# Third attention layer: raw keys loaded in a head's second step, score operands in its third, with the band sum, the values and the masked keys placed anew on GpSimd

## The chip, the cores and the metric

The kernel runs as one program on one core of a Trainium2 chip. The metric is the device time of one execution in microseconds (us). A core has TensorE (PE), VectorE (DVE), ScalarE (ACT), GpSimd (POOL) and SyncE (SP), each with an instruction stream of its own; they meet at semaphores. In this kernel SP issues the DMA transfers, and sixteen DMA engines carry them out.

## The reference

Eight layers one after another work on x, four sequences of 512 tokens with 128 channels: attention and feed-forward in turn, each between layer norms and with a residual. The change touches the third attention layer alone (L2_attn):

```python
qkv = (x @ w_qkv.T).reshape(B, N, 3, H, hd).transpose(2, 0, 3, 1, 4)     # B 4, N 512, H 16, hd 8
q, k, v = (qkv[0] * scale, qkv[1], qkv[2])
attn = jnp.einsum('bhid,bhjd->bhij', q, k)
idx = (clip(j - i, -31, 31) + 31)                                          # 63 buckets
qL = jnp.einsum('bhid,hdm->bhim', q, rpe_k_table)
attn = attn + jnp.take_along_axis(qL, idx, axis=-1)
kL = jnp.einsum('bhjd,hdm->bhjm', k * scale, rpe_q_table)
attn = attn + jnp.swapaxes(jnp.take_along_axis(kL, idx, axis=-1), 2, 3)
attn = jax.nn.softmax(attn, axis=-1)
out = jnp.einsum('bhij,bhjd->bhid', attn, v)
S = segment_sum(attn, idx)                                                 # over j, into 63 buckets
out = out + jnp.einsum('inbh,hnd->bhid', S, rpe_v_table)
return out.transpose(0, 2, 1, 3).reshape(B, N, C) @ w_proj.T + b_proj
```

The relative terms differ from a constant only within 31 tokens of the diagonal, so the kernel computes them on a band of three 32-wide blocks around it.

## The kernel before, in words

`l2_attn` (L2053) works through 16 heads. A head has eight steps (PAIRS = 8), and a step treats two of the sixteen 32-token query blocks of all four sequences at once, 128 partitions by two times 512 keys. Every engine runs its own loop over the step number t, with h = t // 8 the head and i = t % 8 the step in the head, and what each engine does in which step is written out by hand; the text calls (h, i) step i of head h. Only semaphores tie the loops together.

In a step, TensorE computes the scores of two blocks (L2668 to L2673) into one of two PSUM slots, VectorE adds the band `qb` to them (L2523) and takes the maximum (L2525), ScalarE exponentiates them into `pr` (L2606), and VectorE transposes the probabilities of the step before (L2532). Three steps and more later TensorE multiplies them with the values (L2702). The band of a head goes three ways round:

- Query side: TensorE (L2636) computes it two heads ahead, ScalarE copies it out (L2585), SP stores it to DRAM (`q_store`, L2373) and loads it back skewed by one element per row (`q_load`, L2380) into `qb`.
- Key side: SP loads the head's eight rows of raw keys, repeated over 16 shifts, into the single buffer `rawk` (`keys`, L2336) and a table of shifts (L2340). GpSimd multiplies the raw keys with a mask into the single buffer `xk` (`expand`, L2462), TensorE multiplies them with the shifts in steps 1 to 3 (L2649), and ScalarE copies the product to `kb` (L2592). `combine` on GpSimd masks the far part of `qb` (L2470) and adds `kb` (L2472).
- Probability side: SP stores the band part of `pr` to DRAM four times a head (`p_store`, L2391 to L2397) and loads it back skewed twice a head (`s_load`, L2404) into `sb`. GpSimd zeroes what lies outside (`cut`, L2477), VectorE transposes it (L2538), TensorE multiplies it with the value table (L2715).

Score operands of a head (`head_scores`, L2347 to L2351: queries and keys split into bf16 parts, and a row of constants) are loaded one head ahead, the value table too (`head_values`, L2357). `values` on GpSimd (L2448, L2452) spreads the next head's values over the four sequences.

All DMAs of the loop are issued by SP on its one queue, in program order, and SP stands still at each wait. Its steps before the change: `p_store` in even steps (it waits for ScalarE), `s_load` in steps 3 and 7 (it waits at L2403 until the store issued three steps earlier has landed), `q_load` of the next head and `q_store` of the one after in step 0, `head_scores` of the next head in step 3, `keys` of head h+2 in step 4 (waits for `xk_ready`, signalled by `expand` of head h+1), `head_values` in step 5. GpSimd's: `sums` in steps 1 and 5, `cut` in 2 and 6, `combine` of the next head in 4, `values` of the next head in 5 (waits for `pv_done`, which TensorE signals in its step 4), `expand` of head h+2 in 7.

The skewed loads read DRAM through

```python
pitch = width + GRP
return bass.AP(band.tensor, band.offset + offset, [[GRP * pitch, B], [pitch + step, GRP], [1, width]])
```

with B = 4 and GRP = 32, while the raw keys' source has 16 as its first dimension: `[[0, HALF], [T * P, HD], [1, T * P]]`.

Of the kernel before, what the change touches and what calls it, by code (L numbers as in the profile page):

```python
# [22 lines left out]
HEADS, HD = 16, 8  # L23
# [2029 lines left out]
def l2_attn(nc, xs, c, w, scratch):  # L2053
# [4 lines left out]
    with ExitStack() as ctx:  # L2058
# [269 lines left out]
        with nc.Block() as block:  # L2328
            @block.sync
            def _(sp):  # L2330
                def keys(h):

                    if h:
                        sp.wait_ge(m["xk_ready"], h)
                    src = bass.AP(k32.tensor, k32.offset + h * HD * T * P, [[0, HALF], [T * P, HD], [1, T * P]])
                    sp.dma_start(rawk[:, :], src).then_inc(m["kl"], 16)  # L2336
                    if h >= 2:
                        sp.wait_ge(m["l_ps"], ROUND["k", h - 2, KEY_ROUNDS - 1])
                    src = bass.AP(rel_d.tensor, rel_d.offset + h * HD * KEY_SHIFTS, [[1, HALF], [KEY_SHIFTS, HD], [1, WINDOW_COLS]])
                    sp.dma_start(kshift[h % 2][:, :], src).then_inc(shifts_loaded[h % 2], 16)  # L2340
# [12 lines left out]
                def head_values(h):  # L2353

                    if h >= 2:
                        sp.wait_ge(m["o_ps"], 2 * h - 2)
                    sp.dma_start(rvt[h % 2][:, :, :].rearrange("p k n -> p (k n)"), rv_d[h]).then_inc(rv_slot_loaded[h % 2], 16)  # L2357
# [24 lines left out]
                def p_store(o):  # L2382
                    n, u = o // 2, 4 * (o % 2)
                    sp.wait_ge(m["p_ready"], 4 * o + 4)
                    if n >= PBAND_RING and o % 2 == 0:
                        before = n - PBAND_RING
                        sp.wait_ge(s_read[before % 2], 16 * (before // 2 + 1))
                    dst = pband[n % PBAND_RING][:, GRP:].rearrange("p (a c) -> p a c", c=BAND)
                    src, sem = pr[o % PR_RING], p_stored[o % PR_RING]
                    if o % 4 == 0:  # L2390
                        sp.dma_start(dst[:, 0, GRP:], src[:, 0, GRP:BAND]).then_inc(sem, 16)  # L2391
                        sp.dma_start(dst[:, 1:4, :], src[:, 1:4, 0:BAND]).then_inc(sem, 16)
                    elif o % 4 == 3:
                        sp.dma_start(dst[:, u:u + 3, :], src[:, 0:3, 0:BAND]).then_inc(sem, 16)
                        sp.dma_start(dst[:, u + 3, 0:2 * GRP], src[:, 3, 0:2 * GRP]).then_inc(sem, 16)
                    else:
                        sp.dma_start(dst[:, u:u + 4, :], src[:, :, 0:BAND]).then_inc(sem, 16)  # L2397

                def s_load(n):
                    for o in (2 * n, 2 * n + 1):  # L2400
                        sp.wait_ge(p_stored[o % PR_RING], p_stores(o))
                    if n >= 2:
                        sp.wait_ge(m["st_ready"], n - 1)  # L2403
                    sp.dma_start(sb[n % 2][:, :, :].rearrange("p a n -> p (a n)"), skewed(pband[n % PBAND_RING], 1, 1, HROW)).then_inc(s_read[n % 2], 16)  # L2404
# [14 lines left out]
                for t in range(L2_STEPS + 4):  # L2419
                    h, i = t // PAIRS, t % PAIRS  # L2420
                    if t % 2 == 0 and 0 <= (t - 2) // 2 < L2_STEPS // 2:
                        p_store((t - 2) // 2)
                    if t % 4 == 3 and 0 <= (t - 7) // 4 < 2 * HEADS:
                        s_load((t - 7) // 4)
                    if i == 0 and h + 1 < HEADS:
                        q_load(h + 1)
                    if i == 0 and 3 <= h + 2 < HEADS:
                        q_store(h + 2)
                    if i == 3 and 2 <= h + 1 < HEADS:
                        head_scores(h + 1)  # L2430
                    if i == 4 and h + 2 < HEADS:
                        keys(h + 2)
                    if i == 5 and 2 <= h < HEADS:
                        head_values(h)

            @block.gpsimd
            def _(g):
                g.memset(ones3[:, :], 1.0).then_inc(m["ones_ready"], 1)
                g.memset(xk[:, 0:GRP], 0.0).then_inc(m["once_ready"], 1)
                g.memset(xk[:, GRP + T * P:], 0.0).then_inc(m["once_ready"], 1)  # L2440

                def values(h):

                    if h:
                        g.wait_ge(m["vd_ready"], h)
                    if h >= 2:
                        g.wait_ge(m["pv_done"], 2 * h - 2)
                    g.tensor_tensor(vs[:, :, :, :], va[:, :, h, :].unsqueeze(1).broadcast_to([P, 2, NB, HD]),  # L2448
                                    rvf[:, :, h, :].unsqueeze(2).broadcast_to([P, 2, NB, HD]), ALU.add).then_inc(m["vs_ready"], 1)
                    g.wait_ge(m["vs_ready"], h + 1)  # L2450
                    for v in range(2):
                        last = g.tensor_tensor(vd[h % 2][:, v, :, :].rearrange("p k (b d) -> p k b d", d=HD),  # L2452
                                               vs[:, v, :, :].unsqueeze(2).broadcast_to([P, NB, B, HD]),
                                               of_batch.unsqueeze(1).unsqueeze(3).broadcast_to([P, NB, B, HD]), ALU.mult)
                    last.then_inc(m["vd_ready"], 1)

                def expand(h):

                    g.wait_ge(m["kl"], 16 * (h + 1))
                    if h:  # L2460
                        g.wait_ge(m["l_ps"], ROUND["k", h - 1, KEY_ROUNDS - 1])
                    g.tensor_tensor(xk[:, GRP:GRP + T * P].rearrange("p (g c) -> p g c", c=HALF), rawk[:, :].rearrange("p (g c) -> p g c", c=HALF),  # L2462
                                    own_shift.unsqueeze(1).broadcast_to([P, T * P // HALF, HALF]), ALU.mult).then_inc(m["xk_ready"], 1)

                def combine(h):

                    g.wait_ge(qband_read[h % 2], 16 * (h // 2 + 1))
                    g.wait_ge(m["l_ready"], ROUND["k", h, KEY_ROUNDS - 1])
                    far = qb[h % 2][:, :, 2 * GRP:]
                    g.tensor_tensor(far, far, reached.unsqueeze(1).broadcast_to([P, NB, GRP]), ALU.mult).then_inc(m["added"], 1)  # L2470
                    g.wait_ge(m["added"], h + 1)
                    g.tensor_tensor(qb[h % 2][:, :, :], qb[h % 2][:, :, :], kb[:, :, :], ALU.add).then_inc(m["comb_ready"], 1)  # L2472

                def cut(n):

                    g.wait_ge(s_read[n % 2], 16 * (n // 2 + 1))
                    g.tensor_tensor(sb[n % 2][:, :, 0:GRP], sb[n % 2][:, :, 0:GRP], inside.unsqueeze(1).broadcast_to([P, NB // 2, GRP]),  # L2477
                                    ALU.mult).then_inc(m["masked"], 1)

                def sums(n):  # L2480

                    g.wait_ge(m["p_ready"], 8 * n + 8)
                    if n >= 4:
                        g.wait_ge(m["u_ps"], n - 3)
                    g.tensor_tensor(sm[:, n % 4, :, :, :], rs[:, n % 2, :].rearrange("p (g a) -> p a g", a=NT).unsqueeze(3).broadcast_to([P, NT, 2, B]),
                                    of_batch.unsqueeze(1).unsqueeze(1).broadcast_to([P, NT, 2, B]), ALU.mult).then_inc(m["sm_ready"], 1)

                expand(0)
                values(0)
                combine(0)  # L2490
                expand(1)
                values(1)
                for t in range(L2_STEPS + 12):
                    h, i = t // PAIRS, t % PAIRS
                    if t % 4 == 1 and 0 <= (t - 5) // 4 < 2 * HEADS:
                        sums((t - 5) // 4)
                    if t % 4 == 2 and 0 <= (t - 10) // 4 < 2 * HEADS:
                        cut((t - 10) // 4)
                    if i == 4 and h + 1 < HEADS:
                        combine(h + 1)  # L2500
                    if i == 5 and 2 <= h + 1 < HEADS:
                        values(h + 1)
                    if i == 7 and h + 2 < HEADS:
                        expand(h + 2)
                ln.powers(g, 2 * B, start=B)

# [780 lines left out]
```

## Time and profile before

| | us |
|---|---|
| median of 3 runs | 2629.41 (2624.09 to 2635.16) |
| profiled execution | 2632.55 |
| its span, first to last instruction | 2630.6 |
| PE / DVE / ACT / POOL busy | 1926.2 / 1713.3 / 1090.8 / 847.6 |
| the layer's stage, about | 1555 to 2085 |

A line of instruction groups gives busy time, mean duration and idle time before them, with what ended it. In the waits, "A <- B" means that A stood idle until B's result came. The DMA share is the mean busy share of the sixteen DMA engines. A DMA issued by SP counts from its issue to its landing, when its semaphore is complete; a DMA "issue" on SP takes about half a microsecond of SP itself.

### The profile page before, as it was taken

How to read it: one execution, taken by the hardware profiler on the slowest of the kernel's cores; microseconds unless marked ns; L12 is line 12 of the kernel's file. 1: busy time of each engine (PE TensorE's matmuls, PEld its weight loads, DVE VectorE, ACT ScalarE, POOL GpSimd, SP SyncE). 2: the span in 40 equal slices, each digit the busy share in tenths (PEclk: the TensorE clock that was granted, in tenths of full speed). 3: DMA queues.
4: the chain of work that ended last, by engine and by line, in shares of the span. 5: the costliest groups of instructions: out<-in, count | busy, mean ns of one | idle time of the engine just before them, and what ended most of it. 6: DMA issues, size and time to landing. Idle time of an engine off the chain costs nothing. (4 is left out here: it accounts for less than half of the span.)

```text
span 2630.6 us, 46533 instructions
## 1 busy us (share of the span) xinstructions
PE 1926.2 (73%) x16472; PEld 1324.4 (50%) x16472; DVE 1713.3 (65%) x4060; ACT 1090.8 (41%) x2021; POOL 847.6 (32%) x627
## 2 busy tenths in 40 slices
PE   4888886387777784559999647787787549995446
PEld 1555554155555553437777524454454338884334
DVE  3777776576555554659999843788888672224564
ACT  1666663254544442204444223555555213331332
POOL 3000000574444421014444334445545169201001
PEclk8999999699999987659999765898988669997667
DMA  3011110210000000010000065566665140000000
GB/s 100 29 38 39 39 39 3 63 27 15 15 15 15 15 15 5 1 21 11 20 20 20 11 192 140 164 177 172 173 173 153 48 175 17 16 0 8 0 1 19
DMA packets 126467, 145.04 MB, mean 55 GB/s; under 512 B 72472, under 2 KB 100171, under 8 KB 123490
## 3 DMA queue, kind: packets, MB, share of 16 engines
q1 hardware_dynamic: 123040, 132.95, 18.1%
q10 hardware_dynamic: 3266, 9.96, 1.0%
q8 instruction: 99, 1.62, 0.3%
q14 instruction: 62, 0.51, 0.1%
HBM read 94.59 MB, written 40.81 MB: 51 GB/s over the span
## 5 line engine op out<-in xcount | busy, mean ns | idle before, releaser
L407 ACT ACTIVATE l0a_pr<-l0a_sm,l0a_nm 128x512 f32<-128x512 f32 x256 | 184.9, 723 | 147.4 <-DVE l0a_nm L324 146.9
L324 DVE CUSTOM_DVE_ANT_0 l0a_sm<-l0a_ps_s,l0a_tb 128x512 f32<-128x512 f32 x256 | 171.0, 685 | 93.9 <-PE l0a_ps_s L473 90.8
L2606 ACT ACTIVATE l2a_pr<-l2a_ps_s,l2a_nm 128x512 f32<-128x512 f32 x256 | 174.1, 687 | 120.8 <-DVE l2a_nm L2525 119.9
L481 PE MATMUL l0a_ps_p<-top_c_ident,l0a_pr 128*128 128x128 f32 x1024 | 170.4, 290 | 54.2 <-ACT l0a_pT L415 54.1
L481 PEld LDWEIGHTS l0a_ps_p<-top_c_ident,l0a_pr 128*128 128x128 f32 x1024 | 110.0, 143 | 117.1 <-ACT l0a_pr L407 64.7
L2525 DVE TENSOR_REDUCE l2a_nm<-l2a_ps_s 128x2 f32<-128x1024 f32 x128 | 156.7, 1224 | 4.4
L2532 DVE STREAM_TRANSPOSE l2a_tt<-l2a_pr 128x1024 f32<-128x1024 f32 x128 | 158.0, 1234 | 0.1
L1508 POOL TENSOR_TENSOR l1f_h<-l1f_lm,l1f_sg 128x512 f32<-128x512 f32 x72 | 92.6, 1286 | 184.0 <-DVE l1f_lm L1577 184.0
L754 POOL TENSOR_TENSOR l0f_ct<-l0f_raw,l0f_cos_scaled 128x1024 f32<-128x1024 f32 x32 | 76.3, 2386 | 184.1 <-issue 94.7
L1880 ACT ACTIVATE l2f_h<-l2f_ps_h 128x512 f32<-128x512 f32 x128 | 76.7, 599 | 134.7 <-PE l2f_ps_h L1425 128.9
L1635 ACT ACTIVATE l1f_csb<-l1f_ps_c,l1f_b3e 128x512 f32<-128x512 f32 x128 | 88.2, 689 | 104.9 <-PE l1f_ps_c L1425 104.6
L1918 PEld LDWEIGHTS l2f_ps_y<-l2f_w2T,l2f_h 128*128 128x128 f32 x1024 | 119.1, 192 | 2.6
L2702 PE MATMUL l2a_ps_o<-l2a_tt,l2a_vd 128*32 128x256 f32 (+7 forms) x1472 | 119.8, 364 | 0.0
L1918 PE MATMUL l2f_ps_y<-l2f_w2T,l2f_h 128*128 128x128 f32 x1024 | 119.3, 275 | 0.0
L1838 DVE SCALAR_TENSOR_TENSOR l2f_acc<-l2f_ps_y,l2f_comb,l2f_acc 128x128 f32<-128x128 f32 x112 | 31.6, 344 | 133.1 <-PE l2f_ps_y L1918 132.9
L990 PE MATMUL l0f_ps_side<-l0f_wqkv,l0f_hT 128*128 128x512 f32 x192 | 109.8, 663 | 11.5 <-ACT l0f_hT L905 10.8
L2523 DVE TENSOR_TENSOR l2a_ps_s<-l2a_ps_s,l2a_qb 128x192 f32<-128x192 f32 (+2 forms) x160 | 45.7, 303 | 106.2 <-PE l2a_ps_s L2673 61.3
L286 POOL COPY l0a_vh<-l0a_va 128x128 f32 x14 | 4.1, 296 | 333.2 <-PE l0a_ps_o L492 333.2
L473 PE MATMUL l0a_ps_s<-l0a_ks,l0a_qs 48*128 48x512 bf16 x256 | 101.7, 398 | 10.1 <-issue 9.5
L2649 PE MATMUL l2a_ps_l<-l2a_xk,l2a_kshift 128*32 128x256 f32 x768 | 71.3, 504 | 48.7 <-POOL l2a_xk L2462 46.2
L770 POOL TENSOR_TENSOR l0f_rn<-l0f_ss,top_c_half 128x16 f32<-128x16 f32 x32 | 95.0, 2968 | 33.1 <-DVE l0f_ss L854 32.1
L2462 POOL TENSOR_TENSOR l2a_xk<-l2a_rawk,l2a_masks 128x2048 f32<-128x2048 f32 x16 | 72.3, 4517 | 66.0 <-DMA l2a_rawk<-l_k 66.0
(501 smaller groups left out, 5220.9 us busy)
## 6 DMA issues: line engine op xcount, KB each, us to landing
l2a_rawk<-l_k SPq DMA_DIRECT2D x16, 1024.0 KB, 13.2
l2a_qb<-l_qband SPq DMA_DIRECT2D x16, 768.0 KB
l2a_sb<-l_pband SPq DMA_DIRECT2D x32, 384.0 KB
l_qband<-l2a_staged SPq DMA_DIRECT2D x14, 768.0 KB, 15.4
l0a_tb<-l_bias SPq DMA_DIRECT2D x16, 448.0 KB
l2a_ks<-l_k SPq DMA_DIRECT2D x16, 384.0 KB
l_pband<-l2a_pr SPq DMA_DIRECT2D x32, 192.0 KB, 9.4
l_pband<-l2a_pr SPq DMA_DIRECT2D x32, 144.0 KB, 2.9
```

Source lines behind the costliest of these rows:

```text
L324: v.tensor_tensor_reduce(sm[j % 4][:, :], ps_s[j % 2][:, :], tb[slot][:, off:off + N][:, ::-1], -1.0, 3e38, ALU.add, ALU.min, nm[:, j % 4: ...
L407: a.activation(pr[j % 4][:, :], sm[j % 4][:, :], ACT.Exp, bias=nm[:, j % 4:j % 4 + 1], scale=-1.0).then_inc(m["p_ready"], 1)
L473: pe.matmul(ps_s[j % 2][:, :], qs[slot][:, b * N + it * P:b * N + (it + 1) * P], ks[slot][:, b * N:(b + 1) * N], start=True, stop=True).th ...
L481: last = pe.transpose(ps_p[j % 2][:, tile(k)], pr[j % 4][:, tile(k)], ident[:, :])
L770: g.tensor_tensor(rn[:, u, :], ss[:, u, :], c["half"][:, :], ALU.pow).then_inc(m["rn_ready"], 1)
L990: last = pe.matmul(bank[:, :], hT[:, tile(t)], wqkv[:, l, i * F_INNER:(i + 1) * F_INNER], start=True, stop=True)
L1508: g.tensor_tensor(h[b % 2][:, k, :], lm[:, k, :], sg[:, k, :], ALU.mult).then_inc(h_ready, 1)
L1918: last = pe.matmul(ps_y[b % 2][:, t, :], h[b % 2][:, k, t * P:(t + 1) * P], w2T[slot][:, k, :], start=(k == 0), stop=(k == FC - 1))
L2525: v.tensor_reduce(nm[:, g % 2, :], ps_s[g % 2][:, :, :], AX, ALU.max, negate=True).then_inc(m["nm_ready"], 1)
L2532: v.transpose(tt[n % 2][:, u * NB:(u + 2) * NB, :].rearrange("p (u k) i -> p u (k i)", u=2), pr[g // 2 % PR_RING][:, 2 * (g % 2):2 * (g % ...
L2606: a.activation(pr[slot][:, 2 * (g % 2) + u, :], ps_s[g % 2][:, u, :], ACT.Exp, bias=nm[:, g % 2, u:u + 1], accum_out=rs[:, n % 2, 2 * (g % ...
L2702: last = pe.matmul(ps_o[n % 2][GRP * g:GRP * (g + 1), (lo - a0) * GRP:(hi - a0) * GRP], vd[h % 2][:, v, k, :], tt[n % 2][:, block:block + ...
```

## The change

On SP, `keys` of head h+2 moves from step 4 to step 1, and `head_scores` of head h+1 from step 3 to step 2. On GpSimd, `values` moves from step 5 to step 3, `combine` from step 4 to step 5, and `expand` from step 7 to step 6; within a step their order behind `sums` and `cut` stays, and `values` now comes ahead of `combine`. Nothing else differs.

```diff
                     if i == 0 and 3 <= h + 2 < HEADS:
                         q_store(h + 2)
-                    if i == 3 and 2 <= h + 1 < HEADS:
+                    if i == 1 and h + 2 < HEADS:
+                        keys(h + 2)
+                    if i == 2 and 2 <= h + 1 < HEADS:
                         head_scores(h + 1)
-                    if i == 4 and h + 2 < HEADS:
-                        keys(h + 2)
                     if i == 5 and 2 <= h < HEADS:
                         head_values(h)
...
                         cut((t - 10) // 4)
-                    if i == 4 and h + 1 < HEADS:
+                    if i == 3 and 2 <= h + 1 < HEADS:
+                        values(h + 1)
+                    if i == 5 and h + 1 < HEADS:
                         combine(h + 1)
-                    if i == 5 and 2 <= h + 1 < HEADS:
-                        values(h + 1)
-                    if i == 7 and h + 2 < HEADS:
+                    if i == 6 and h + 2 < HEADS:
                         expand(h + 2)
```

## Rows read from the trace of the kernel before

**Rows 1.** The page: span, and busy time of each engine

```profile
span 2630.6 us, 46533 instructions
PE 1926.2 (73%) x16472; PEld 1324.4 (50%) x16472; DVE 1713.3 (65%) x4060; ACT 1090.8 (41%) x2021; POOL 847.6 (32%) x627
```

**Rows 2.** L2462 (first and last start), and the engines' busy time in 342 us

```profile
L2462 POOL TENSOR_TENSOR l2a_xk<-l2a_rawk,l2a_masks x13: 4502/4517/4531, 1672.4 to 2013.8; 128x2048 f32<-128x2048 f32 x13
...
1672.40:2014.40 342.00, 270.79 (x3933) 158.20 (x3932) 284.07 (x382) 181.22 (x488) 166.35 (x121) 0.87 0.62 173
```

**Rows 3.** Who waited for whom, 1672.4 to 2014.4: total us, times, longest

```profile
POOL l2a_xk L2462 <- DMA l2a_rawk<-l_k: 55.3, 13, 5.4
DVE l2a_ps_s L2523 <- PE l2a_ps_s L2673: 52.9, 30, 4.5
...
PE l2a_ps_l L2649 <- POOL l2a_xk L2462: 37.8, 12, 5.0
...
PE l2a_ps_s L2668 <- DMA l2a_ks<-l_g: 11.1, 8, 3.0
...
DVE l2a_st L2538 <- POOL l2a_sb L2477: 0.5, 1, 0.5
```

**Rows 4.** DMA busy share in tenths, 40 slices of 1818 to 1847 us

```profile
DMA  9832322222662769742895999997983232248299
```

**Rows 5.** Windows: stretch, length, busy PE, PEld, DVE, ACT, POOL, clock, DMA share, GB/s

```profile
1642.20:1643.20 1.00, 1.00 (x24) 0.42 (x24) 1.00 (x1) 0.00 (x0) 0.88 (x2) 1.00 0.19 46
1820.50:1824.50 4.00, 4.00 (x48) 1.63 (x44) 1.37 (x2) 2.21 (x6) 0.54 (x1) 0.50 0.27 99
1812.00:1814.00 2.00, 0.65 (x15) 0.17 (x15) 2.00 (x3) 1.40 (x4) 0.00 (x0) 1.00 0.27 110
1588.50:1591.50 3.00, 2.43 (x12) 2.19 (x11) 0.00 (x0) 0.48 (x1) 0.91 (x1) 0.50 1.00 254
1804.50:1808.50 4.00, 3.79 (x45) 2.68 (x43) 3.93 (x6) 3.33 (x11) 3.32 (x5) 1.00 1.06 192
1817.50:1818.80 1.30, 0.00 (x0) 0.00 (x0) 1.30 (x2) 0.00 (x0) 1.30 (x1) 1.00 1.03 421
2048.20:2049.40 1.20, 1.20 (x12) 0.62 (x4) 1.17 (x3) 0.53 (x2) 0.00 (x0) 0.50 0.24 33
2049.40:2052.00 2.60, 1.24 (x20) 0.51 (x19) 2.60 (x4) 1.45 (x4) 0.24 (x1) 0.50 0.26 98
2059.60:2060.30 0.70, 0.70 (x13) 0.34 (x4) 0.70 (x2) 0.38 (x1) 0.00 (x0) 1.00 1.00 277
```

**Rows 6.** DMA issues, 1672.4 to 2014.4: count, KB each, us to landing

```profile
l2a_rawk<-l_k SPq DMA_DIRECT2D x12, 1024.0 KB, 13.4
l_qband<-l2a_staged SPq DMA_DIRECT2D x12, 768.0 KB, 15.5
l2a_sb<-l_pband SPq DMA_DIRECT2D x24, 384.0 KB
```

**Rows 7.** VectorE's timeline at 1843.8 us: the first addition of a head

```profile
1843.77 0.39 DVE L2523 TENSOR_TENSOR l2a_ps_s<-l2a_ps_s,l2a_qb 128x64 f32<-128x64 f32 x2
```

**Rows 8.** SP's timeline, 1797 to 1832 us

```profile
1815.31 1.64 SPq L2373 DMA_DIRECT2D l_qband<-l2a_staged  x1
...
1825.81 1.43 SPq L2347 DMA_DIRECT2D l2a_qs<-l_q  x1
...
1831.51 0.57 SPq L2336 DMA_DIRECT2D l2a_rawk<-l_k  x1
```

**Rows 9.** GpSimd's timeline, 1800 to 1845 us

```profile
1829.67 1.28 POOL L2470 TENSOR_TENSOR l2a_qb<-l2a_qb,l2a_masks 128x512 f32<-128x512 f32 x1 [8.63 <-ACT l2a_kb L2592]
1831.03 3.45 POOL L2472 TENSOR_TENSOR l2a_qb<-l2a_qb,l2a_kb 128x1536 f32<-128x1536 f32 x1
```

**Rows 10.** SP's own waits, 1672.4 to 2014.4; a store's landing, 2005 to 2080

```profile
SPq L2403 <- DMA l_pband<-l2a_pr: 51.6, 12, 6.5
...
l_pband<-l2a_pr SPq DMA_DIRECT2D x5, 144.0 KB, 2.0
```

## The prediction

> **What bounds the stage now.** The page first: of 2630.6 us VectorE is busy 65% and TensorE 73%, so no engine bounds the whole [rows 1]; the change touches one stage, so I cut that out. In its steady part the masked keys of 13 heads start between 1672.4 and 2013.8 us: 12 periods of 28.45 us. VectorE is busy 284.07 of those 342 us, 23.7 us a head; 4.8 us a head is idle [rows 2]. The waits say who is late: VectorE waits 52.9 us for the scores (L2673), TensorE 37.8 us for GpSimd's masked keys (L2649 on L2462), GpSimd 55.3 us for the raw keys' DMA, and 11.1 us goes on the score operands' DMA [rows 3]. Read that way, two late loads cost nearly all the idle time, and an earlier issue cures it.
>
> I don't stop there, because the next view is of the DMA itself. In one head (1818 to 1847 us) the DMA share is never under two tenths, and falls to two again and again [rows 4]. Two tenths have a meaning. `skewed()` builds the source of the query band load (L2380) and of the probability band load (L2404) with B=4 as its outermost dimension. While only the query band load is in flight the share is 0.27 at 99 GB/s; while only the band of probabilities is, 0.26 at 98 GB/s; stores over all engines reach 421 GB/s at 1.03 [rows 5]. So the skewed loads run on four of sixteen engines, and a share that never drops below a quarter means those four never rest. I checked the other heads' slices for the same floor; the row shown stands for them. All DMAs go through SP's queue; what SP issues later stands behind on each engine.
>
> **The four engines' budget of a head.** Sizes from [rows 6], the smaller ones by their shapes in the code, rates from [rows 5]:
> - query band load: 786 kB at 99 GB/s, 7.9 us.
> - two band loads: 393 kB at 98 GB/s, 4.0 us each, 8.0 us.
> - query band store: 786 kB over sixteen at 421 GB/s, 1.9 us.
> - a sixteenth of raw keys, shifts and score operands (1049+57+393+197+25 kB, 108 kB an engine); the tail of the keys on the four alone goes at 110 GB/s, 27.5 an engine: 3.9 us.
> - four probability stores, some 750 kB in small runs; such a store runs at about 277 GB/s: 2.7 us.
> - contention: with twelve engines on the raw keys and four on a band load, share 1.06 gives only 192 GB/s, 12 an engine. The twelve carry 786 kB of keys at 144 GB/s in 5.5 us; the four carry 264 kB meanwhile, clean 2.7 us: 2.8 us lost.
>
> Sum 27.2 us of 28.45. The rest may be slow starts (a band load's first 1.2 us after idleness go at 33 GB/s [rows 5]). The period is the four engines' queue; VectorE's 23.7 us lies inside it. The late keys are where the queue presents its bill.
>
> **The change, part by part.** No byte, instruction or wait is added or removed.
>
> (a) Raw keys and shifts, SP step 4 to step 1. Two DMAs, about 0.6 us of SP each; in the row they are issued at 1831.51, and their new place is right behind the query band store of 1815.31 [rows 8], some 14 us earlier, before the stores of steps 2 and 4, the operands and the band load of step 3. The keys' wait of 4.3 us a head on GpSimd goes.
>
> (b) Score operands, step 3 to 2: three DMAs, the first 1.43 us of SP [rows 8], now ahead of the band load of step 3. With (a), that load stands behind 1.7 MB more; on the four engines this is 3.9 us. It was 1.9 MB deep, and now meets all but the last probability store and itself.
>
> (c) What is late next: the band load of step 3 is wanted by cut() in GpSimd's step 6, then by VectorE's transposition in step 7 (L2538). GpSimd runs in order and expand() moves to step 6, behind that cut(). So when the band is late, the 4.5 us masking of keys is too, SP's keys() waits for it (L2336 waits for xk_ready), and TensorE's L2649 at the next step 1. VectorE waits now 0.5 us for cut() [rows 3]; I expect some 4 us a head there in place of the 4.4 us on scores (52.9 in 12 heads).
>
> (d) values() from step 5 to 3: it waits for pv_done, which TensorE signals in step 4. GpSimd blocks about a step; behind it are sums() and combine(). vd is needed a head later. combine() at step 5 instead of 4: 1.28+3.45 us [rows 9], wanted 2 to 3 steps later. Now it starts 14.1 us ahead of the head's first addition (1829.67 against 1843.77) [rows 7, 9]. Both I cost at nothing; without that cover they would cost at most a step, an eighth of the period, 3.6 us a head.
>
> (e) A gap. In step 7 SP waits for the landing of the store of step 4 before it may issue the second band load (L2403, 51.6 us in 12 heads [rows 10]). Now the raw keys stand behind that store and keep the four engines fed. After the change only the small store of step 6 and the rvt load do: about 0.9 us. Among idle engines a 144 KB store takes 2.0 us from issue to landing [rows 10], 0.5 of it transport (147 kB at 277 GB/s), so 1.5 for first byte and receipt, which is also what lies between one DMA's last byte and the first of the next that had to wait for it; 0.1 is my estimate from landing to issue. The gap is then 1.6-0.9=0.7 us. If the load also starts slowly as it does after idleness, 0.8 us more (1.2 us at 33 instead of 98 GB/s [rows 5]), and with nothing queued behind 2.4 in all. Bounds: 0 (there is no gap now to win back) and 2.4 us a head; I take 0.7, because the engines come from a running store and not from idleness.
>
> (f) Contention moves: the raw keys now meet the query band load, not a band load. No row shows that pair. Bounds: loss 0 (the load is not slowed) and 3.6 us (all of keys and operands at half rate); I take 2.8 as for the band load, which is the nearest row: same four engines, same direction.
>
> The raw keys alone on sixteen engines move at 254 GB/s, against 421 for stores [rows 5]; so reading the keys is slow by itself, and a load beside them likely pays. That it doesn't pay is rival B. The Trainium skill (HBM Reference, Specifications) states that a core that streams alone measures about 425 GB/s; by that, the keys of twelve engines and the query band would fit together and the loss in (f) would be 0, as in rival B. The row at 254 GB/s disagrees, and the measurement decides.
>
> On (e), the skill (DMA: Bandwidth & Descriptors, Anatomy of one DMA) gives a fixed cost of about 2.0 us for a DMA, mostly the write's receipt. By that the gap would be 1.1 us rather than 0.7, and the sum 5 us higher.
>
> **Sum.** Per head: +0.7 (gap) +0 (contention only moved), over 13 heads +9.1 us; in the first two heads, where the four engines do rest (share 0.19 from 1642.2 to 1643.2 us [rows 5]), earlier keys save 1 to 2 us. Together +7.6. The profiled execution took 2632.55 us (span 2630.6, 2 around it); its forecast is 2640. It stood 3.1 over the median 2629.41, so against the median: 2637.
>
> **Rivals.**
> A (forecast): the four engines stay the bound; waits move from the keys to the band load. 2637, own range 2622 to 2648. For: the floor of two tenths and a budget that comes within 1.3 us.
> B: the query band load is not slowed by the keys. Loss 2.8 goes, gap 0.7 to 1.5 comes: -1.3 to -2.1 a head, 13 heads, -17 to -27: about 2607. For: larger runs, another place in DRAM. Against: 254 and 192 GB/s whenever keys are read.
> C: the four are no bound, and the earlier issue does what the waits promise. TensorE's 37.8 and the operands' 11.1 us vanish: with first heads about -50: 2580; VectorE's idle 58 us is its limit. Against: the floor.
> D (slower): at L2403 SP finds the queue drained, the four idle and restart slowly at each head's second band load. It decides from the point where the store of step 4 is the last large thing in the queue. +1.5 to +2.4 a head over 13: +20 to +31, about 2654. For: after each idle stretch the rows show this slow start. Against: the stores of step 4 and 6 are issued early and lie in the queue together.
> That the change does not do what it says is inside A: expand() is placed a step earlier yet stands behind cut(), so the masked keys need be no earlier.
>
> **Chances.** About 0.5% (13 us) is what a measurement here can tell from no change. A 0.48, B 0.20, C 0.08, D 0.24. Of A 0.38 lies within 13 us, 0.02 below and 0.08 above. Faster: B+C+0.02=0.30; same 0.38; slower D+0.08=0.32. The range, 2598 to 2657, holds A, B and most of D; it leaves out C, the end of D and what I did not think of.
>
> **What would show it.** Right: period 28 to 30 us; DMA share again never under two tenths, or with one short dip a head just before the second band load; no GpSimd wait on raw keys; new waits of GpSimd's cut() on the band load and of VectorE on it; (f) is right if the window with keys and query band shows about 190 to 200 GB/s. Wrong: share falling under two tenths for microseconds while the period is 25 us (C), or a query band load as fast as 99 GB/s beside the keys (B). D: a dip of over 1 us in each head, and L2403 as long as now.

## The result, and the profile after

The changed kernel takes 2697.13 us (median of 4 runs, 2691.47 to 2699.59) against 2629.04 us: ratio 1.0255, 95% interval 1.0228 to 1.0282, 68 us slower and 40 us above the upper end of the range. The profiled execution took 2699.59 us. No engine does more than before; the page has the same instructions and nearly the same busy times as [rows 1], in a longer span:

```profile
span 2697.7 us, 46533 instructions
PE 1923.8 (71%) x16472; PEld 1324.6 (49%) x16472; DVE 1715.9 (64%) x4060; ACT 1088.6 (40%) x2021; POOL 846.3 (31%) x627
```

The masked keys' first and last start, and the engines' busy time in the same 12 heads (the rows that answer to [rows 2]):

```profile
L2462 POOL TENSOR_TENSOR l2a_xk<-l2a_rawk,l2a_masks x13: 4522/4532/4547, 1667.6 to 2079.4; 128x2048 f32<-128x2048 f32 x13
...
1667.60:2079.40 411.80, 272.97 (x3952) 159.39 (x3952) 287.01 (x384) 180.10 (x488) 165.42 (x122) 0.80 0.58 144
```

A head takes 411.8/12 = 34.3 us where it took 28.45; 5.85 us times 12 is 70 us, so the whole difference arises in this steady part. The granted clock of the stretch fell from 0.87 to 0.80 [rows 2], but TensorE's busy time in it rose by only 2.2 us, so the clock is not the cause. The waits over that stretch, against [rows 3]; the last line of this fence is SP's own wait, against [rows 10]:

```profile
POOL l2a_sb L2477 <- DMA l2a_sb<-l_pband: 113.0, 25, 6.9
...
POOL l2a_vs L2448 <- PE l2a_ps_o L2702: 95.3, 12, 9.9
ACT l2a_pr L2606 <- DMA l_pband<-l2a_pr: 85.9, 12, 9.0
...
PE l2a_ps_s L2668 <- DMA l2a_ks<-l_g: 72.8, 12, 7.8
...
DVE l2a_tt L2532 <- ACT l2a_pr L2606: 61.1, 12, 6.9
...
DVE l2a_st L2538 <- POOL l2a_sb L2477: 46.1, 12, 4.5
...
DVE l2a_ps_s L2523 <- PE l2a_ps_s L2673: 12.9, 18, 1.7
...
SPq L2403 <- DMA l_pband<-l2a_pr: 88.6, 12, 7.9
```

The waits on the raw keys are gone from this list, and of those on the masked keys 0.2 us are left. In their place VectorE waits 3.8 us a head for the band that cut() releases, and 5.1 us for exponentials, which ScalarE holds back because the probability store from the same buffer has not landed. The operands' DMA costs TensorE 72.8 us, where it was 11.1. Apart from the wait of values(), which (d) expected, the large waits that grew lead back to a DMA. The landings tell how (the first line is the kernel before, the others the changed one; KB each, median us from issue to landing):

```profile
l_pband<-l2a_pr SPq DMA_DIRECT2D x24, 144.0 KB, 4.6
```

```profile
l_pband<-l2a_pr SPq DMA_DIRECT2D x24, 144.0 KB, 9.9
...
l2a_rawk<-l_k SPq DMA_DIRECT2D x12, 1024.0 KB, 22.5
```

The probability stores now stand behind the keys, and those of 144 KB land 5 us later; ScalarE waits for that landing, and so does SP before the second band load. The keys themselves take 22.5 us instead of 13.4 [rows 6], which gives back most of the 14 us by which they are issued earlier.

The DMA view of one head, from SP's second band load to the next (1838.8 to 1873 us), busy share in tenths and GB/s. It answers to [rows 4]:

```profile
DMA  0362499699979997952977522222228248222322
GB/s 3 40 176 97 187 435 357 236 274 134 115 96 160 125 110 93 178 146 72 247 149 254 101 43 79 86 86 98 117 117 249 93 147 259 101 97 101 118 91 65
```

The GB/s of the kernel before, for the row in [rows 4]:

```profile
GB/s 415 335 103 95 116 93 93 102 102 103 202 178 93 198 229 238 293 127 67 256 302 164 271 191 174 205 236 139 190 218 124 102 111 87 70 138 238 102 407 407
```

Two things are new. The row begins with a 0: the four engines rest, which they hardly did before. And in the tenth to the sixteenth slice, where the keys and the query band load are under way on nearly all engines (nines and sevens), only 93 to 160 GB/s move; in the sevens, eights and nines of the kernel before, stores aside, it was 139 to 302. The windows show both, against [rows 5] (share and GB/s are the last two columns): first the keys beside the query band load, in two heads; then the tail of the queue on four engines, as quick as ever; then the pause at the second band load.

```profile
1813.00:1817.00 4.00, 4.00 (x80) 2.46 (x71) 3.59 (x5) 3.11 (x10) 0.73 (x1) 1.00 0.95 143
1847.00:1851.00 4.00, 4.00 (x79) 2.66 (x78) 3.96 (x5) 3.01 (x9) 0.00 (x0) 1.00 1.07 132
1835.00:1836.80 1.80, 0.45 (x8) 0.00 (x0) 0.01 (x1) 0.45 (x2) 0.00 (x0) 0.50 0.26 99
1838.80:1840.30 1.50, 0.40 (x3) 0.20 (x6) 1.39 (x5) 0.00 (x0) 1.50 (x2) 0.50 0.16 12
```

Counted over the packets of SP's queue in the trace, fewer than four are in flight for 2.6 us of each head, and none at all for 1.2 of these; before it was 0.1 us. So of the 5.85 us a head, 2.5 are time in which at least one of the four engines rests, and the other 3.35 are slower work on the same bytes. The trace doesn't say which engine carries a packet, so this division is not exact: averaged over four places, the rest is 1.8 us.

### The profile page after: what moved, and what is told of

Its sections match the earlier page's. It is cut to its first block and busy times, and to the rows that moved or that the text cites. A ratio compares the mean times of both kernels' runs of the same rounds, so it can differ in the third digit from the quotient of the medians.

```text
span 2697.7 us, 46533 instructions
## 1 busy us (share of the span) xinstructions
PE 1923.8 (71%) x16472; PEld 1324.6 (49%) x16472; DVE 1715.9 (64%) x4060; ACT 1088.6 (40%) x2021; POOL 846.3 (31%) x627
## 5 line engine op out<-in xcount | busy, mean ns | idle before, releaser
L2636 PE MATMUL l2a_ps_l<-l2a_tabq,l2a_q 128*128 128x96 f32 x512 | 85.8, 320 | 8.0 <-ACT l2a_pr L2585 3.4
L332 DVE COPY l0a_pT<-l0a_ps_p 128x512 f32<-128x512 f32 x128 | 87.7, 686 | 4.3 <-issue 3.5
```

## The experiments

Each was timed beside the kernel before, whose medians were 2625.6 to 2628.7 us. The period of a head is always from the fourth to the sixteenth start of the masked keys, over 12, and "rest" is the time with fewer than four packets in flight.

### Whose part of the change it is

`sp_only` has only the hunk of the diff in SP, `pool_only` only the one in GpSimd.

> Only SP's part of the change (raw keys in step 1, score operands in step 2); GpSimd as before. Theory T (the queue of the four engines that carry the skewed loads: slower beside the keys, and empty before the second band load): the whole loss is SP's, 2690 to 2705 us. Rival G (GpSimd's new order: masked keys behind cut(), values() waiting for TensorE): 2625 to 2650 us.

> Only GpSimd's part of the change; SP as before. Theory T: the four engines' queue is untouched, 2620 to 2640 us. Rival G: 2670 to 2700 us.

Measured: `sp_only` 2700.43 us, ratio 1.0271 (1.0246 to 1.0296); `pool_only` 2629.95 us, ratio 1.0010 (0.9995 to 1.0026). GpSimd's new order does nothing measurable in the old order of DMAs; the whole loss is in SP's order. The 95 us that GpSimd waits in values() for TensorE are covered.

Then one of SP's two moves at a time, taken back from the changed kernel:

```diff
# after_keys4
-                    if i == 1 and h + 2 < HEADS:
-                        keys(h + 2)
                     if i == 2 and 2 <= h + 1 < HEADS:
                         head_scores(h + 1)
+                    if i == 4 and h + 2 < HEADS:
+                        keys(h + 2)
...
# after_ops3
-                    if i == 2 and 2 <= h + 1 < HEADS:
+                    if i == 3 and 2 <= h + 1 < HEADS:
                         head_scores(h + 1)
```

> The changed kernel with the raw keys back in step 4, the score operands still in step 2. Theory T: keys no longer meet the query band load and again lie behind the store that L2403 waits for, so both parts of the loss go: 2620 to 2645 us. Rival O (the operands ahead of the band load do it): 2670 to 2700 us.

> The changed kernel with the score operands back in step 3, behind the band load, the keys still in step 1. Theory T: the keys make the loss, so most of it stays, 2680 to 2697 us. Rival O: 2625 to 2650 us.

Measured: `after_keys4` 2649.27 us (ratio 1.0090, 1.0066 to 1.0114), `after_ops3` 2703.21 us (1.0295, 1.0271 to 1.0319). With the operands left in step 3 the keys' move alone costs 73 us (`after_ops3` against `pool_only`), with them in step 2 it costs 48. The operands' move costs 19 us while the keys are in step 4 (4 us over what I expected at most) and nothing once the keys are in step 1. The two do not add. In `after_keys4` a head takes 29.65 us with 0.95 us of rest. Its DMA share from 1780 to 1813 us keeps the floor of two tenths but for one slice, near the end:

```profile
DMA  2283279722222237899722969999898943222218
```

### Slow reading beside the keys

The keys' source repeats a head's eight rows for sixteen shifts, so that all engines read the same 64 KB. `after_rows` and `before_rows` read 128 different rows instead; the bytes and their places in SBUF are the same.

```diff
-                    src = bass.AP(k32.tensor, k32.offset + h * HD * T * P, [[0, HALF], [T * P, HD], [1, T * P]])
+                    src = bass.AP(k32.tensor, k32.offset, [[HD * T * P, HALF], [T * P, HD], [1, T * P]])
```

> The changed kernel, but the raw keys' load reads 128 different rows of the key tensor instead of the head's eight rows sixteen times over; same bytes, same places in SBUF, so the keys are the wrong ones. Theory T1 (sixteen engines reading the same eight rows are slow and slow the query band load beside them; the empty queue is the rest): the 3 us a head of slow reading go, 2645 to 2665 us. Theory T2 (any reading of this much beside the query band load is as slow; the rows don't matter): 2690 to 2700 us.

> The kernel before with the same edit of the keys' source (wrong keys). T1: the loss of 2.8 us a head that the prediction counted goes too, 2585 to 2605 us. T2: 2620 to 2635 us.

Measured: `after_rows` 2665.36 us (ratio 1.0143, 1.0126 to 1.0160), 32 us under the changed kernel, period 31.3 us. `before_rows` 2616.10 us (0.9957, 0.9940 to 0.9973), only 12 us under the kernel before, where I had expected 25 or more. In `after_rows` the keys beside the query band load move at 220 GB/s, not 143:

```profile
1801.00:1805.00 4.00, 4.00 (x78) 2.46 (x71) 3.93 (x6) 3.22 (x10) 0.22 (x1) 1.00 1.01 220
```

Reading the same rows over and over is therefore a part of the loss: with different rows the two orders are 49 us apart instead of 68. T1 holds in kind and not in size, for it had left both kernels without slow reading.

### The empty queue

`after_fill` puts work behind the store that SP waits for:

```diff
-                    if i == 0 and 3 <= h + 2 < HEADS:
-                        q_store(h + 2)
...
                         head_values(h)
+                    if i == 6 and 3 <= h + 2 < HEADS:
+                        q_store(h + 2)
```

> The changed kernel with the query band store moved from step 0 to step 6, behind the probability store, so that the four engines have 1.9 us of work while SP waits at L2403. If the empty queue costs 2 to 3 us a head: 2660 to 2675 us. If the slow reading alone makes the loss: 2690 to 2705 us.

Measured: 2686.30 us (ratio 1.0228, 1.0211 to 1.0245), 11 us under the changed kernel and 11 over the upper end of what I expected. The rest fell from 2.6 to 0.8 us a head, the period only from 34.3 to 32.7. The DMA share from 1835 to 1869 us no longer has a zero:

```profile
DMA  2912227997898999995622222228342822599321
```

So the empty queue is real. Its price is 1.6 us a head by the two traces, whose executions are 17 us apart, and 0.8 us a head by the medians, 11 us apart. Either is less than the 1.8 us of rest that went, so some of it comes back as slower work. The edit also takes the store away from behind the query band load; what that alone does is not measured.

Both cures at once:

> Both cures at once on the changed kernel: the keys read from 128 different rows (wrong keys), and the query band store in step 6. If slow reading and empty queue are separate terms that add: 2640 to 2660 us (2697 - 32 - 11 = 2654). If they are one and the same: 2660 to 2670 us.

Measured: 2655.08 us (ratio 1.0106, 1.0063 to 1.0150). 2697 less 32 less 11 is 2654: by the medians the two terms add, within the interval of some 11 us either way. By the periods they do not quite: 34.3 less 3.0 less 1.6 is 29.7 us, and the trace has 30.75. And 39 us still stood between this and `before_rows`, so one more pair asks where they come from. From head 1 on it loads only the first quarter of each raw key row; the rest of the buffer keeps old keys.

```diff
-                    sp.dma_start(rawk[:, :], src).then_inc(m["kl"], 16)
+                    cols = T * P if h == 0 else T * P // 4
+                    src = bass.AP(k32.tensor, k32.offset + h * HD * T * P, [[0, HALF], [T * P, HD], [1, cols]])
+                    sp.dma_start(rawk[:, 0:cols], src).then_inc(m["kl"], 16)
```

> The kernel before, but from head 1 on only a quarter of each raw key row is loaded (512 of 2048 columns; the rest of the buffer keeps old keys). A quarter of the keys' own time on the four engines (1.8 us less) and of the 2.8 us lost beside them (2.1 us less): period 24.5 us, near VectorE's 23.7, 2572 to 2595 us by both theories.

> The changed kernel with the same quarter of the keys. If the keys' bytes beside the query band load make the rest of the loss (they are in flight there a quarter of the time): own bytes 1.8 and three quarters of some 6 us slow reading go, leaving the empty queue, period 27 to 28.5 us, 2600 to 2625 us. If the order by itself does it: the distance to the other order stays near 68 us, 2640 to 2665 us.

Measured: `before_quarter` 2595.39 us (ratio 0.9876, 0.9857 to 0.9896), period 26.15 us where I expected 24.5; `after_quarter` 2622.98 us (0.9982, 0.9969 to 0.9995), period 28.1 us. The distance between the two orders falls from 68 to 28 us. With three quarters of the keys' bytes goes 40 us of the difference, so the keys' bytes make most of it and the order by itself the smaller part. What is left is 2.0 us a head; rest is 2.75 us a head against 1.4 there, which explains 1.4 of the 2.0.

### Are the four engines the bound at all?

Everything so far rests on the reading that the skewed loads run on four engines. `before_split` issues each as four DMAs, one a sequence, whose outermost dimension is 32 rows; the waits on their semaphores count 16*B.

```diff
-                    return bass.AP(band.tensor, band.offset + offset, [[GRP * pitch, B], [pitch + step, GRP], [1, width]])
+                    return bass.AP(band.tensor, band.offset + offset + b * GRP * pitch, [[pitch + step, GRP], [1, width]])
...
-                    src = skewed(qband[h % QBAND_RING], GRP - 1, -1, ROW)
-                    sp.dma_start(qb[h % 2][:, :, :].rearrange("p a n -> p (a n)"), src).then_inc(qband_read[h % 2], 16)
+                    for b in range(B):
+                        src = skewed(qband[h % QBAND_RING], GRP - 1, -1, ROW, b)
+                        sp.dma_start(qb[h % 2][GRP * b:GRP * (b + 1), :, :].rearrange("p a n -> p (a n)"), src).then_inc(qband_read[h % 2], 16)
```

> The kernel before with each skewed load issued as four DMAs, one for each sequence, 32 rows each, so that all sixteen engines carry it; same bytes. If the four engines' queue is what bounds this stage: the period falls towards VectorE's 24 us, 2565 to 2590 us. If it does not bound it (the waits on the keys and operands are latency, rival C of the prediction), or SP's twelve more DMAs a head cost as much: 2620 to 2660 us.

Measured: 2558.75 us, ratio 0.9741 (0.9720 to 0.9761): 69 us faster than the kernel before. The stretch of 12 heads is 291.5 us, VectorE busy in 283.84 of them, and its waits there are two lines:

```profile
1649.30:1940.80 291.50, 248.66 (x3977) 152.18 (x3968) 283.84 (x385) 180.90 (x489) 165.16 (x121) 0.96 0.82 203
```

```profile
DVE l2a_ps_s L2526 <- PE l2a_ps_s L2676: 2.9, 4, 1.6
DVE l2a_ps_s L2526 <- issue: 0.2, 1, 0.2
```

A head takes 24.3 us, VectorE's work 23.7. That the split load runs on more than four engines shows where it is in flight alone: the band load of probabilities has a DMA share of 0.81 at 212 GB/s, where [rows 5] had 0.26 at 98.

```profile
1662.00:1663.00 1.00, 1.00 (x29) 0.52 (x22) 0.52 (x2) 0.00 (x0) 0.00 (x0) 1.00 0.81 212
```

The DMA view of the 12 heads shows what follows: the raw keys land after 9.3 us instead of 13.4 [rows 6] and the query band store after 5.8 instead of 15.5, because nothing has a tail on four engines any more. A quarter of the band takes 3.6 us.

```profile
l2a_rawk<-l_k SPq DMA_DIRECT2D x12, 1024.0 KB, 9.3
l2a_qb<-l_qband SPq DMA_DIRECT2D x48, 192.0 KB, 3.6
l_qband<-l2a_staged SPq DMA_DIRECT2D x12, 768.0 KB, 5.8
```

The same edit on the changed kernel:

> The changed kernel with each skewed load issued as four DMAs of 32 rows, over all sixteen engines. If the order of SP's DMAs only matters because four engines carry the skewed loads: VectorE bounds this one too, 2550 to 2575 us, and the 68 us between the two orders are gone. If the slow reading beside the keys and the empty queue cost by themselves, whatever the engines: 2590 to 2640 us.

Measured: 2557.54 us (ratio 0.9734, 0.9693 to 0.9775). The two orders now cost the same; 68 us of difference are 1. This is the version that beats both, in either order.

Which of the loads counts:

> The kernel before with only the two loads of the probability band a head split over all engines, the query band load left on four. The four engines then lose 8 us of band loads and the 2.8 us those lost beside the keys, and get back 1.9: 19.5 us a head, under VectorE's 23.7, so VectorE bounds: 2555 to 2580 us. If the query band load still binds: 2590 to 2620 us.

> The kernel before with only the query band load split over all engines, the two probability band loads left on four. Splitting the band loads alone gave 15 us of the 69; there the keys, the operands and the stores of steps 2 and 4 still stood behind the query band's 8 us on four engines. If that tail ahead of the others is what holds them: most of the 69 comes here, 2560 to 2585 us. If the four engines' total only matters, each load in proportion to its bytes: about as much as for the band loads, 2600 to 2615 us.

Measured: the two band loads alone 2613.28 us (ratio 0.9940, 0.9921 to 0.9959), the query band load alone 2591.44 us (0.9860, 0.9825 to 0.9896). They carry the same number of bytes a head, but give 15 and 35 us, and both together 69. My budget had left the engines at 19.5 us a head with the band loads split, and the period came to 27.4 with 1.7 us of rest. So the four engines' total is not the whole rule. The same trace still has GpSimd waiting for the raw keys and for the query band, which both stand in or behind the 8 us on four engines:

```profile
POOL l2a_qb L2477 <- DMA l2a_qb<-l_qband: 84.4, 8, 13.6
...
POOL l2a_xk L2469 <- DMA l2a_rawk<-l_k: 41.5, 13, 5.2
```

## Why the prediction was wrong

**What held.** The bound was named rightly: not an engine, and not the two late loads, but the queue of four DMA engines. `before_split` shows it, and it refutes rival C. The waits moved as (c) said: VectorE waits 3.8 us a head for cut() where I had written some 4. But (c) did not have the larger wait, 5.1 us a head on exponentials behind the late probability store, and its wait of TensorE at L2649 did not come (0.2 us in all). GpSimd's moves, (d), cost nothing (`pool_only`). Rival D, the queue found empty at L2403, is what happened, from the place that it named, though SP's wait there, which D had as long as before, rose from 51.6 to 88.6 us. Rival B fell: the query band load is slowed by the keys, and more than the band load was.

**The step that failed first is (f).** I took 2.8 us a head for the contention, "as for the band load", and moved it over unchanged, with 3.6 us as the upper bound. But the old row was a row of a different pair: keys beside a band load ran at 192 GB/s in sum, keys beside the query band load at 143 and 132. By the prediction's own way of counting, twelve engines at 107 GB/s need 7.3 us for the 786 kB of keys, the four carry 262 kB meanwhile, clean 2.6: 4.7 us lost; in the other window 5.3. That is 1.9 to 2.5 us a head more than I took, and above my bound (also above the 3.9 us that my own budget has for keys, shifts and operands). "Half rate" was no bound; it was the one ratio that I had seen. The packets of all 12 heads agree with the two windows: one of the raw keys (8 KB) takes 649 ns on average where it took 559, one of the query band (6 KB, load and store together) 352 where it took 246, and one of a band load (3 KB), which no longer meets the keys, 142 where it took 170. The quarter runs tie this to the keys' bytes (40 us of the difference between the orders), and the runs with other rows tie 19 us of the difference to the repetition of rows. Why this pair reads worse than the other is open.

**The second is (e).** I took 0.7 us of rest with 2.4 as the end, and measured 2.5. In the changed kernel's trace the first packet of the second band load starts 1.3 us after its issue in every head, with nothing of size in flight between. The slow start after a pause, which I left to rival D, comes every head too: of the first eight packets at least one takes 0.46 to 1.0 us, where 0.12 us is usual. The window at 12 GB/s holds both. `after_fill` prices what it removes of this at 0.8 to 1.6 us a head.

**The third is in the bounds.** I gave a price to each unknown alone and let D stand with the contention at its old value. The loss is both at once: some 2.2 us of slower reading of keys and query band, 2.5 of rest, and about 1 for the operands, which (b) priced at nothing though their bytes too now meet the query band load (`after_keys4`: 0.9 us a head against `pool_only`, with the keys where they were). That makes 5.7 of the 5.85 us. It is an account and not a measurement: what the runs took away one by one is 32 us (other rows), 11 us (the filled queue) and 40 us (three quarters of the keys' bytes), and these overlap. The operands' share is carried over from another order, though, and with the keys in step 1 taking their move back gave no gain, so the last term is not measured in place. A range that took the upper ends together, 2.4 and 0.8 us over 13 heads, would have reached about 2670, still short.

The rules of the Trainium skill did not change the outcome. The rate of about 425 GB/s that the Trainium skill (HBM Reference, Specifications) gives for a core alone pointed at no loss in (f) and was far off here, at 132 to 143 GB/s. The fixed cost of about 2 us that the Trainium skill (DMA: Bandwidth & Descriptors, Anatomy of one DMA) gives is stated there for DMAs that GpSimd issues, and these are SP's. It pointed the right way for (e), 1.1 us instead of 0.7 (1.2 with the 0.1 us that the sum has from landing to issue), and was still short of 2.5.

## What to carry to other kernels

Before a load is issued earlier, look whether the DMA share ever falls to zero. Here a floor at a quarter was four engines that never rest, and the earlier issue only reordered their queue. Count the engines that a transfer uses by its outermost dimension, and mend that first; here it was worth 69 us on the kernel before and 140 us on the changed one, while the order by itself was worth 68 us in the wrong direction. And a DMA that waits for another's landing needs something queued in between, though here that gave back only 11 us.

## What the runs showed of the hardware that I had not expected

SP was held at the issue itself. The first of the operands' DMAs took SP 0.5 to 2.7 us before the change and 4.9 to 7.0 us after it, when the keys are issued ahead of it (durations are minimum, median and maximum in ns; the first line is the kernel before, the second the changed one):

```profile
L2347 SPq DMA_DIRECT2D l2a_qs<-l_q x13: 524/1775/2732, 1683.5 to 2023.3; - x13
```

```profile
L2347 SPq DMA_DIRECT2D l2a_qs<-l_q x12: 4886/5735/7014, 1676.5 to 2054.8; - x12
```

The semaphore that stands before this issue is not the cause: it tells of scores whose maxima q_load() has already waited for in step 0. The median falls to 0.5 us with the keys back in step 4 (`after_keys4`), to 2.2 with a quarter of their bytes and to 3.4 with other rows, so the hold goes with the keys that are queued and with how slowly they move. All of SP's issues together took 10.1 us a head before and 22.0 after. It looks like a limit on what may be queued, but no run isolates it, and it can be the effect of the slow reading rather than a cost of its own.

Reading the same eight rows from all engines is slower than reading 128 rows (143 against 220 GB/s beside the query band load; over the 12 heads a packet of the keys takes 649 against 490 ns). What is read at the same time is slower too: 352 against 314 ns for a packet of the query band, load and store together.
